# Dense stages in scaled fp16 pairs from chunk 3 on, with scales taken on the chip, in a fused residual block with a recurrence

## What is computed

```python
# layer 0: c = layernorm(cond); w = gelu(c @ W1 + bias1) @ W2 + bias2; a1, b1, a2, b2 = w split, each (B, D, 8)
u   = einsum('btd,bdr->btr', x, a2)
mid = gelu(x @ base_down + einsum('btr,blr->btl', u, b2))
v   = einsum('blr,btl->btr', b1, mid)
x   = x + (x + mid @ base_up.T + einsum('bkr,btr->btk', a1, v))
# layer 1: h(0) = cond
xW  = x @ Wx + b
h(t) = tanh(xW[:, t] + h(t-1) @ Wh)          # 512 steps, one after the other
y   = x + h
```

## Time and profile before

| | us |
|---|---|
| median of three runs | 1222.71 |
| the profiled execution | 1217.61 |
| its span, first to last instruction | 1215.6 |
| PE busy | 1189.0 |
| DVE busy | 868.0 |
| ACT busy | 626.7 |
| POOL busy | 254.5 |

### The profile page before, as it was taken

How to read it: one execution, slowest core, us unless ns; L and a number is a source line. 1 busy time by engine, 2 the same in 40 slices (tenths; PEclk the granted TensorE clock), 3 DMA queues, 4 the chain that set the end, 5 groups by cost and what they waited for, 6 DMA issues and landing times.

```text
span 1215.6 us, 50835 instructions
## 1 busy us (share of the span) xinstructions
PE 1189.0 (98%) x21046; PEld 964.5 (79%) x21046; DVE 868.0 (71%) x3648; ACT 626.7 (52%) x2648; POOL 254.5 (21%) x523
## 2 busy tenths in 40 slices
PE   8987999999999999999999999999999999999998
PEld 8544888888888888888888888888888888888776
DVE  4533577777777777777777777777777777777676
ACT  4121555556555555555555556555565556555433
POOL 0000122222222222222222222222222222222211
PEclk8988999999999999999999999999999999999999
DMA  9988211312121211213121212213122212102021
GB/s 312 393 338 310 37 20 24 51 20 45 30 38 23 41 30 33 43 20 51 24 38 32 34 28 34 42 20 53 22 37 36 35 24 38 20 3 38 2 46 28
DMA packets 260565, 75.73 MB, mean 62 GB/s; under 512 B 247952, under 2 KB 248096, under 8 KB 260336
## 3 DMA queue, kind: packets, MB, share of 16 engines
q1 hardware_dynamic: 258112, 72.35, 25.0%
q10 hardware_dynamic: 2224, 0.14, 0.2%
HBM read 55.68 MB, written 16.78 MB: 60 GB/s over the span
## 4 chain that ended last, share of the span: by engine, by line
PE 91%; DMA 4%; ACT 2%; DVE 1%; issue 1%; SPq 0%; POOLq 0%; POOL 0%
PE bulk L1074 47%; PE rec L1090 34%; PE bulk L1077 5%; DMA work<-in_L_cond_W_dram 4%; PE bulk L1063 2%; PE bulk L1052 2%; ACT rec L598 1%; DVE z L924 1%; ACT hf L678 1%; PE bulk L1235 0%; PE rec L977 0%; PE bulk L1203 0%; DVE wx_s L742 0%; SPq L488 0%; PE rec L1074 0%
## 5 line engine op out<-in xcount | busy, mean ns | idle before, releaser
L1090 PEld LDWEIGHTS rec<-hs,wh_s 128*128 128x128 f16 x16352 | 442.8, 96 | 130.8 <-DVE hs L932 127.9
L1090 PE MATMUL rec<-hs,wh_s 128*128 128x32 f16 x16352 | 493.4, 177 | 3.9 <-ACT rec L598 2.0
L555 POOL TENSOR_TENSOR work<-work,hf 128x64 f32<-128x64 f32 x512 | 253.1, 494 | 956.4 <-DVE hs L932 955.5
L678 ACT ACTIVATE hf<-z 128x32 f32<-128x32 f32 x1024 | 218.4, 230 | 451.8 <-DVE z L924 445.9
L924 DVE TENSOR_REDUCE z<-rec 128x32 f32<-128x96 f32 x1022 | 234.0, 258 | 176.7 <-PE rec L1090 170.3
L1074 PE MATMUL bulk<-mid_s,up_s 128*128 128x512 f32 x768 | 222.6, 410 | 0.5 <-ACT mid_s L639 0.5
L932 DVE SCALAR_TENSOR_TENSOR hs<-hf,hs 128x32 f16<-128x32 f32 x1022 | 196.5, 192 | 35.3
L1074 PE MATMUL bulk<-act_x,down_s 128*128 128x512 f32 x768 | 218.6, 408 | 0.0
L929 DVE TENSOR_SCALAR hs<-hf 128x32 f16<-128x32 f32 x1022 | 181.9, 178 | 50.9 <-ACT hf L678 4.8
L1074 PE MATMUL bulk<-act_s,wx_s 128*128 128x512 f32 x756 | 207.1, 406 | 0.0
L598 ACT ACTIVATE rec<-work 128x32 f32<-128x32 f32 x1022 | 185.3, 213 | 0.0
(11 more groups left out here) (129 smaller groups left out, 692.0 us busy)
## 6 DMA issues: line engine op xcount, KB each, us to landing
work<-in_L_cond_W_dram SPq DMA_DIRECT2D x33, 1024.0 KB, 8.8
out_dram<-work SPq DMA_DIRECT2D x240, 64.0 KB, 2.5
work<-in_x_dram SPq DMA_DIRECT2D x224, 64.0 KB, 4.0
work<-in_x_dram SPq DMA_DIRECT2D x8, 256.0 KB, 9.8
work<-in_L_cond_base_up_dram SPq DMA_DIRECT2D x1, 1024.0 KB, 8.2
work<-in_L_cond_base_down_dram SPq DMA_DIRECT2D x1, 1024.0 KB, 14.5
wh_f<-in_L_cond_Wh_dram SPq DMA_DIRECT2D x1, 1024.0 KB, 17.0
work<-in_L_cond_Wx_dram SPq DMA_DIRECT2D x1, 1024.0 KB, 8.0
```

What stands on the lines that cost most here:

```text
L555: nc.gpsimd.tensor_tensor(to, xs, hf[:, t % 4], ALU.add).then_inc(sum_done, 1)
L678: nc.scalar.activation(hf[:, t % 4, half], z[:, half], ACT.Tanh, scale=inv_reg).then_inc(tanh_done, 1)
L1090: last = nc.tensor.matmul(R[fo][:, m, 0:PARTS, :], wh_s[:, q, k, n * P:(n + 1) * P], hs[:, k, :, :], start=(m == k == q == 0), stop=(k == ...
```

## The change

**fp16 pairs.** For chunks n >= 3 (F16_FROM) the activations and the three dense weights are split into fp16 HI and LO parts in place of fp32r ones. The passes, the number of products and their columns are the same. The rank products, u and v stay in fp32 types. The fp16 tensors x16, g16, h16, up16, wx16, down16 lie over the memory of the fp32r ones, and the freed halves hold a fourth x1 buffer, so x1[n % 3] becomes x1[n % 4].

**Scales.** fp16 has a small range, so each operand is multiplied by a power of two. Bounds are computed per chunk on the chip, for three quantities: x, the input of gelu, and the input of the second layer. For each, ACT sums absolute values along the columns (`accum_out`), POOL takes the maximum over the 128 partitions (`partition_all_reduce`) and combines bounds with small one-column operations, DVE cuts the result to a power of two (`power`), and POOL makes the scales (`cs`). x: slots -15 and -12. u: slots 0 and 2. g: slots 12 and 15. Once, at steps 3 and 9 of chunk 0, the same is done for the weights, from seven maxima that DVE takes (`top_of`).

**Conversion.** From step 42 to 77 the weights are rewritten in place as fp16 pairs by 36 ACT and 24 POOL operations of 512 columns.

**Smaller ones.** The recurrence's products of a step are reordered: half of quadrant (1, 0) now comes after quadrant (0, 1), so that the first sum's input is complete four products sooner. Wx is loaded to another place and later in the start (after W2 piece 13, into wh_f). For n >= 3, POOL doubles x1 (eight operations of 256 columns in slots 24 to 31), which DVE's scalar_tensor_tensor did before on the way. HI of mid is a scaled copy of gel and no longer a second gelu. The rounding of the rank operand moves from DVE to ACT. The three unused products of the last chunk are fp16.

```diff
+F16_FROM = 3
+XT16_AT, XT16_FIRST = (-31, -30, -19, -18), (-21, -20, -19, -18)
+XSUM_AT, XSUM_FIRST = (-30, -29, -18, -17), (-19, -18, -17, -16)
+XTOP_AT, XSCALE_AT = -15, -12
+UTOP_AT, USCALE_AT = 0, 2
+GTOP_AT, GSCALE_AT = 12, 15
...
+            def x_top(n):
+                pool.wait_ge(xsum_done, KT * (n - F16_FROM + 1))
+                link(nc.gpsimd.partition_all_reduce(xtop[:], xsum[:], P, bass.bass_isa.ReduceOp.absmax))
+                link(nc.gpsimd.tensor_tensor(xr[:, 0:2], xtop[:, 0:2], xtop[:, 2:4], ALU.add))
+                link(nc.gpsimd.tensor_tensor(xr[:, 0:1], xr[:, 0:1], xr[:, 1:2], ALU.add))
+                nc.gpsimd.tensor_scalar(xr[:, 0:1], xr[:, 0:1], LEAST, None, ALU.max).then_inc(x_topped, 1)
...
+                    if c + 1 < NC:
+                        other(c + 1, t)
+                    if c + 2 < NC:
+                        other(c + 2, t - TC)
...
+                if n >= F16_FROM and r == XSCALE_AT:
+                    dve.wait_ge(x_topped, n - F16_FROM + 1)
+                    power(xr[:, 2:3], xr[:, 0:1]).then_inc(x_powered, 1)
+                if n >= F16_FROM and r == USCALE_AT:
+                    dve.wait_ge(u_topped, n - F16_FROM + 1)
+                    power(ur[:, 2:3], ur[:, 0:1]).then_inc(u_powered, 1)
+                if n >= F16_FROM and r == GSCALE_AT:
+                    dve.wait_ge(g_topped, n - F16_FROM + 1)
+                    power(gr[:, 2:3], gr[:, 0:1]).then_inc(g_powered, 1)
...
-                    nc.scalar.copy(act_x[:, HI, k], x1[n % 3][:, k]).then_inc(xhi_done, 1)
+                    if n >= F16_FROM:
+                        act.wait_ge(xscale_done, n - F16_FROM + 1)
+                        nc.scalar.activation(x16[:, HI, k], x1[n % 4][:, k], ACT.Copy, scale=scale_of(n, S_X)).then_inc(xhi_done, 1)
...
-                    dense(mid, i, at["mid_banks"], down_s, act_x, b2_s, mid_mm)
+                    dense(mid, i, at["mid_banks"], *((down_s, act_x) if n < F16_FROM else (down16, x16)), b2_s, mid_mm)
...
-                        quadrant(1, 0)
+                        quadrant(1, 0, (0,))
                         pe.wait_ge(h_done, 2 * n)
                         quadrant(0, 1).then_inc(rec_mm, 1)
+                        quadrant(1, 0, (1,))
                         quadrant(1, 1).then_inc(rec_mm, 1)
```

More of the change, by code:

```diff
@@ L131 @@
 WH_HI_AT, WH_LO_AT = 8, 9
-WX_HI_AT, WX_LO_AT = 12, 13
+WX_HI_AT, WX_LO_AT = 20, 21
+WX_LOAD_AFTER = 13
 TURN_AT = 36
@@ L287, in build @@
         rec_mm = sem("rec_mm")
+        tops_done = sem("tops_done")
+        pchain = sem("pchain")
+        k16_done = sem("k16_done")
+        w_topped = sem("w_topped")
+        w_powered = sem("w_powered")
+        x_topped = sem("x_topped")
+        x_powered = sem("x_powered")
+        usum_done = sem("usum_done")
+        u_topped = sem("u_topped")
+        u_powered = sem("u_powered")
+        uscale_done = sem("uscale_done")
+        g_topped = sem("g_topped")
+        g_powered = sem("g_powered")
+        conv_act = sem("conv_act")
+        conv_sub = sem("conv_sub")
+        conv_done = sem("conv_done")
+        xsum_done = sem("xsum_done")
+        gsum_done = sem("gsum_done")
+        xscale_done = sem("xscale_done")
+        gscale_done = sem("gscale_done")
+        doubled = sem("doubled")
         y_done = sem("y_done")
@@ L494, in _ @@
             sp.dma_start(wh_f, wh.rearrange("(k p) n -> p k n", p=P)).then_inc(wh_in, 16)
-            for e in range(W2_ENTRY, HALVES + 3):
+            for e in range(W2_ENTRY, W2_ENTRY + HALVES):
                 load(e)
+                if e == WX_LOAD_AFTER:
+                    sp.wait_ge(wh_split, 1)
+                    sp.dma_start(wx_f, wx.rearrange("(k p) n -> p k n", p=P)).then_inc(wx_in, 16)
             sp.wait_ge(x_pe, KT)
@@ new lines, in other @@
+            def other(n, r):
+                if n < F16_FROM:
+                    return
+                if r == XTOP_AT:
+                    x_top(n)
+                if r == XSCALE_AT:
+                    x_scales(n)
+                if r == UTOP_AT:
+                    mid_top(n)
+                if r == USCALE_AT:
+                    mid_scales(n)
+                if r == GTOP_AT:
+                    state_top(n)
+                if r == GSCALE_AT:
+                    state_scales(n)
+                j = r - DOUBLE_AT
+                if 0 <= j < 2 * KT:
+                    if j == 0:
+                        pool.wait_ge(x1lo_done, (n + 1) * KT)
+                    part = x1[n % 4][:, j // 2, j % 2 * (COLS // 2):(j % 2 + 1) * (COLS // 2)]
+                    nc.gpsimd.tensor_tensor(part, part, part, ALU.add).then_inc(doubled, 1)
@@ L910, in _ @@
                     split_weight(1, wx_f, wx_s)
+                for j in tile_at(TOPS_AT, i):
+                    top_of(j)
                 dense_slot(0, i)
@@ L915, in chunk @@
                     n = c * TC + t
+                    if n == 1:
+                        top_of(len(TOPS_AT))
+                    if n == W_SCALE_AT:
+                        dve.wait_ge(w_topped, 1)
+                        power(w_pow[:], w_top[:]).then_inc(w_powered, 1)
                     for f in range(2):
@@ L1081, in dense, with quadrant @@
                     mm.then_inc(done, 1)
-            def quadrant(fo, fi):
-                for m in range(HT):
+            def quadrant(fo, fi, rows=range(HT)):
+                for m in rows:
                     for k in range(fi * HT, (fi + 1) * HT):
@@ L1151, in dense_slot @@
                         pe.wait_ge(fac_split, KT + m + 1)
-                    dense(out, i, at["out_banks"], up_s, mid_s, a1_s, out_mm)
+                    dense(out, i, at["out_banks"], *((up_s, mid_s) if n < F16_FROM else (up16, g16)), a1_s, out_mm)
                 for i in xw_plan[1].get(r, ()):
```

307 lines of the change are left out of this document (273 added, 34 removed).

## The result

| | us | ratio to before, 95% interval |
|---|---|---|
| before (four runs) | 1222.6 | |
| changed (four runs) | 1607.1 (1592.4 to 1609.0) | 1.312 [1.308, 1.317] |
| forecast | 1634, range 1340 to 1880 | |

The change makes the kernel 31% slower. The profiled execution of the changed kernel has a span of 1606.7 us, before it was 1215.6, so 391 us were added.

What follows compares the result with a forecast made beforehand. PE's load was taken to bound chunks 1 to 14. From 1217.6 us profiled: -60 - 3 + 2 + 374 + 4 + 94 = 1629, and 5.1 us for the runs' median gives 1634 us, range 1340 to 1880.

Steps and rivals of the forecast that it cites:

- fp16 on PE, 13 chunks: Chunks 3 to 15: cheaper dense products and no 0.09 us on each step's first one, 4.6 us a chunk, 60 us saved.
- order of products: Reordered recurrence quadrants let z start 0.10 us sooner; worth nothing while PE bounds, 3 us saved in the last chunk.
- conversion: Rewriting the weights as fp16 adds one ACT operation in 36 steps: 2 us more.
- DVE stopped by POOL: At `power`, DVE waits for POOL's three reductions a chunk: 28.8 us a chunk, 374 us over 13 chunks.
- weights' reduction: At step 3 it keeps POOL about 14 us against some 10 us of allowed lag: 4 us more.
- clock behind the stops: PE falls to 1.2 GHz after each of 39 stops; two slow steps, 2.4 us each time: 94 us, bounds none to 234.
- PE's load bounds before, fp16 lowers it: Chunks 1 to 14: PE's 2.04 us a step exceeds the loop's 1.83; with fp16 a five-product step takes 1.90.
- the other ACT and DVE work: Extra sums, about 6 us a chunk on ACT, and DVE work are hidden by the PE step: costed at nothing.
- The standstills: DVE, and with it z, tanh, hs and PE, stops per reduction: x 8.8, u 10.4, g 9.6 us.
- The price of a change of set: Each change of POOL's routine set around a reduction fetches code: 6.4 us, between bounds of 0.01 and 8.8.
- The rival with a costless change: Changing POOL's set costs nothing, DVE never waits and the fp16 gain stands alone: 1162 us, chance 0.18.
- the turning point: Price of one set change at which the DVE stops, 4.6 us a chunk, eat the 61 us gain: 2.4 us.

Runs made afterwards that it cites:

- own sums: Changed kernel with the 39 reductions over partitions replaced by a one-column POOL copy, so each partition scales by its own sum: 1174.6 us, ratio 0.961.
- PE kept at work: Changed kernel plus unused 512-column fp16 products on PE (44, 44 and 28) behind steps 2, 15 and 20: 1561.8 us, ratio 1.279.
- the two versions with the maximum on PE: Changed kernel with PE and DVE making the maximum over partitions instead of POOL: 1196.1 us with the new product order, 1195.5 with the old.

## Why the prediction was right, step by step

| term | forecast | measured | from |
|---|---|---|---|
| fp16 on PE, 13 chunks | -60 | -54 | 67.90 to 63.75 us a chunk, own sums |
| order of products | -3 | about -1 | last chunk, kernel before with it |
| conversion | +2 | about +8 | own sums: chunk 1 71.1 against 67.9, chunk 2 68.9 against 63.75 |
| DVE stopped by POOL | +374 | +375.7 | waits of the changed kernel |
| weights' reduction | +4 | +6 | chunk 0: 78.8 against 72.8 |
| clock behind the stops | +94 | +45 to 50 | PE kept at work |

Chunk 2 already multiplies in fp16 (for chunk 3), so it is compared with a middle chunk of the run with own sums; its extra time lies in steps 0 to 16, and the conversion ends at its step 13.

**PE's load bounds before, fp16 lowers it.** Right. The product at 0.217 us and the vanished 0.09 are in the trace as forecast. A chunk gains 4.15 us where 4.6 were forecast. Some steps are no longer covered by PE; step 9, for example, takes 2.48 us without any reduction and took 2.14 before. That the other ACT and DVE work cost nothing was thus not quite right.

**The standstills.** Right in mechanism, and in sum to 2 us, but two errors are hidden in the sum. The changes of set were taken at 6.4 each and are 6.2 and 7.4, so POOL is away longer; g's standstill is 11.3 us where 9.6 was forecast, u's 10.6 against 10.4. In return x's is 7.0 and not 8.8: its cover is more than three steps of 1.9 us, since steps 17 to 19 take 3.20, 2.15 and 1.88 us in chunk 6, the first of them slow behind g's standstill.

**The price of a change of set.** The 6.4 us were the middle of two loads, since code had to come to POOL "by a transfer of a size that no row shows". The number came out near (6.2 and 7.4), but no run shows such a transfer. In the stretch 693.72:706.40, which holds the end of one change and the whole of the other, the DMA moves 0 GB/s. The DMA queues for instructions (packets, MB, share) moved this in the changed kernel

```profile
q8 instruction: 166, 2.72, 0.8%
q14 instruction: 73, 0.60, 0.2%
```

and this in the run with own sums, which has 78 changes fewer.

```profile
q8 instruction: 166, 2.72, 1.1%
q14 instruction: 72, 0.59, 0.2%
```

So 78 changes of set add one packet to what the profile records. A transfer outside these records can't be excluded; what fills the 6 to 7 us stays open, and that the middle of two loads was near it is luck. The Trainium skill's 5.95 us for the first call to a freshly loaded kernel (GPSIMD Engine Reference, section 2.1 Instruction dispatch) is near the 6.2 of the change to the set with the reduction. Here each of the 39 changes to that set paid it, and the change back to the standard set, for which the section gives no price of its own, paid more.

**The rival with a costless change** rested on L532's 11 ns. It falls: rows of 11 ns stand in front of 6 us. The prediction's reason against it, that the row of before leaves the resident set as it is, fits this. Where it works out the turning point, g's standstill at 2.4 us a change is 1.6 and not 1.4, which makes 4.8 a chunk and leaves the turning point at 2.4.

**The clock.** This is the term that was mis-sized, by a factor of two. The clock fell as forecast, behind each standstill, but I took two slow steps for each of the 39; the recovered 45 to 50 us are 1.2 to 1.3 us a standstill, one slow step of five products. Part of the time at the low clock lies inside the standstill, where nobody needs PE (0.69 in the mean of 693.72:706.40). The experiment may have left a few us of it, as its slow steps 17 and 18 show, but the 57 us beside DVE's waits leave no room for 94.

**The small terms** for the order, the conversion and the weights were each wrong by a factor of 1.5 to 4, with 2 to 6 us each, and all three were set too low. With fp16's 6 us they make 16 us, which cancel a part of the 44 to 49 by which the clock was set too high. The table adds to 382 where 391 were added. The rest of about 9 us is not in the run with own sums, whose span is 39 us below the one of before as the terms without standstills add up to (-41), so it comes with the standstills: it is what is left of the 57 us when the 45 to 50 are taken off. How much of it is the clock is open.

## What to carry to other kernels

Before an operation is put on POOL in a loop, list POOL's instructions in order and count how often the resident routine set changes; each change here was 6 to 9 us of POOL that no busy time shows, and the operation between two of them was 0.4. An engine that looks idle is then no cover: what counts is the slack of the engines that wait for it, here two or three steps at DVE's `power` and the four buffers of hf. Where the reduction is small, a transposition and a product on PE with a maximum on DVE do the same for about 0.5 us of the path each (1.48 us a chunk for three).

## What was not expected

The way back to the standard set (7.4 us) is dearer than the way to the other (6.2). Unused products in a standstill made the changed kernel faster by 45 us, since they kept the clock.

The changes around g's reduction take longest (means 6.8 and 7.9 us). Eleven of its thirteen reductions have thousands of DMA packets beside them, and there the change takes 6.08 to 7.62 us and the change back 7.39 to 8.75; the last two have at most one packet, and take 5.80 and 5.81, and 6.83 and 6.70. So the longer change goes with DMA traffic; no run tests it by itself.

And the start differed between executions: in the two versions with the maximum on PE that differ in the order of products alone, the first tanh began at 137.6 and at 126.4 us. Spans of single executions are therefore compared here by chunks.
